# Batch 0 runs half a stage ahead of batch 1 through the last layers of an eight-layer kernel

## The reference, cut to what matters

```python
# L2x: 16 heads of 8, keys and values from 77 context rows, mask, softmax, then Wo and bias
x = x + tanh(g_xattn[2]) * _L2_xattn_ref(_layernorm(x), ctx, mask, Wq, Wk, Wv, Wo, bo)
# L2f: rows quantised by their own maximum, gate and up (512 wide), silu(gate) * up quantised by row, down
x = x + tanh(g_ffn[2]) * _L2_ffn_ref(_layernorm(x), w_gate, w_up, w_down)
# L3x: one head of 128, 77 context rows
x = x + tanh(g_xattn[3]) * _L3_xattn_ref(_layernorm(x), ctx, ctx, Wq, bq, Wk, bk, Wv, bv)
# L3f: the mean of a batch's rows picks one of 8 experts for the whole batch, then relu MLP 128-512-128
x = x + tanh(g_ffn[3]) * _L3_ffn_ref(_layernorm(x), Wr, br, W1, b1, W2, b2)
```

## Time and profile before

| | |
|---|---|
| time, median of 3 runs | 411.97 us (411.04 to 412.08) |
| the profiled execution | 415.34 us, of which the span of its instructions is 413.6 us |
| busy in the span | PE 295.0 us (71%), DVE 220.8 (53%), ACT 135.2 (33%), POOL 106.4 (26%) |
| mean granted TensorE clock | 0.796 |

### The profile page before, as it was taken

One profiled execution on the slowest core, in us unless ns is written; L12 is line 12 of the kernel. 1 busy time (PEld: TensorE's weight loads), 2 busy tenths in 40 slices (PEclk: granted clock), 3 DMA queues, 4 the chain that ended last, 5 costly groups with the idle time before them and its releaser, 6 DMA issues.

```text
span 413.6 us, 4876 instructions
## 1 busy us (share of the span) xinstructions
PE 295.0 (71%) x1699; PEld 230.0 (56%) x1699; DVE 220.8 (53%) x609; ACT 135.2 (33%) x242; POOL 106.4 (26%) x106
## 2 busy tenths in 40 slices
PE   2879979978858884566998053676999726475396
PEld 1659879568758873334898013233779513254245
DVE  4444542203161014788985369659987588825501
ACT  2220425823221221144443070134454348321150
POOL 4402217603235240224333100412445000000000
PEclk9755755999997898698999655599999966555589
DMA  8970004476765533091000000000000000000001
GB/s 217 339 164 1 0 12 144 155 203 179 238 201 161 175 105 108 3 360 44 0 2 2 0 1 0 0 0 2 1 2 0 2 0 0 1 2 0 0 0 52
DMA packets 21399, 29.72 MB, mean 72 GB/s; under 512 B 3521, under 2 KB 14223, under 8 KB 21376
## 3 DMA queue, kind: packets, MB, share of 16 engines
q1 hardware_dynamic: 19686, 26.66, 21.5%
q0 software_dynamic: 1312, 2.60, 1.9%
q10 hardware_dynamic: 378, 0.16, 0.3%
HBM read 24.74 MB, written 4.67 MB: 71 GB/s over the span
## 4 chain that ended last, share of the span: by engine, by line
PE 43%; DVE 28%; POOL 8%; issue 8%; DMA 7%; ACT 4%; SPq 1%; DVEq 0%; POOLq 0%; ACTq 0%
PE bank L1036 8%; DMA experts<-in_w 5%; POOL xg L558 4%; PE bank L813 4%; PE bank L986 4%; PE bank L978 3%; DVE ln L1210 3%; PE bank L1020 3%; POOL rstd L510 2%; PE bank L1175 2%; DVE pmax L1416 2%; DVE bn L1202 2%; DVE pr L1417 2%; PE bank L1184 2%; PE bank L1018 2%
## 5 line engine op out<-in xcount | busy, mean ns | idle before, releaser
L510 POOL TENSOR_TENSOR rstd<-var,minus_half 128x4 f32<-128x4 f32 x16 | 16.3, 1022 | 112.2 <-DVE var L1207 112.0
L546 POOL TENSOR_TENSOR pr<-pr,psums 128x1232 f32<-128x1232 f32 x12 | 27.0, 2249 | 54.2 <-DVE psums L1427 54.2
L595 ACT ACTIVATE prT<-bank 128x512 f32<-128x512 f32 (+1 forms) x48 | 22.1, 488 | 51.1 <-PE bank L813 50.8
L564 POOL DMA_INDIRECT yt<-acc,experts x23 | 22.5, 980 | 44.4 <-DVE acc L1396 43.0
L978 PE MATMUL bank<-prT,experts 128*128 128x128 f32 x184 | 26.6, 291 | 9.4 <-DMA experts<-in_w 8.7
L1396 DVE COPY acc<-bank 128x128 f32<-128x128 f32 x23 | 6.6, 291 | 46.7 <-PE bank L986 46.6
L1416 DVE TENSOR_REDUCE pmax<-bank 128x6 f32<-128x462 f32 (+1 forms) x48 | 27.4, 571 | 5.4 <-PE bank L1022 3.5
L797 PE MATMUL bank<-ident,ln 128*128 128x128 f32 x40 | 9.5, 383 | 29.1 <-DVE ln L1210 29.1
L978 PEld LDWEIGHTS bank<-prT,experts 128*128 128x128 f32 x184 | 24.0, 204 | 11.2 <-issue 11.2
L986 PE MATMUL bank<-experts,prT 128*128 128x128 f32 x184 | 26.7, 295 | 3.6 <-DVE acc L1396 3.6
L813 PE MATMUL bank<-ident,pr 128*128 128x128 f32 (+1 forms) x140 | 21.7, 290 | 8.2 <-POOL pr L546 7.9
(11 more groups left out here) (282 smaller groups left out, 628.6 us busy)
## 6 DMA issues: line engine op xcount, KB each, us to landing
experts<-in_w SPq DMA_DIRECT2D x23, 512.0 KB, 4.2
experts<-in_w SPq DMA_DIRECT2D x2, 2048.0 KB
xg<-experts SPq DMA_DIRECT2D x1, 1518.0 KB, 10.2
experts<-xg SPq DMA_DIRECT2D x5, 264.0 KB, 5.4
experts<-yt SPq DMA_DIRECT2D x4, 256.0 KB, 3.6
x<-in_x SPq DMA_DIRECT2D x2, 256.0 KB, 3.8
wkv<-in_wk SPq DMA_DIRECT2D x1, 512.0 KB, 6.7
wkv<-in_wv SPq DMA_DIRECT2D x1, 512.0 KB, 6.8
```

The costliest lines, as they stand in the source:

```text
L510: pool.tensor_tensor(rstd[:, b * TB:b * TB + TB], var[:, b, :], minus_half[:, :], ALU.pow).then_inc(rstd_ready, 1)
L546: pool.tensor_tensor(v, v, psums[:, n % 4, 1, :].unsqueeze(2).to_broadcast([P, H, R]), ALU.mult).then_inc(p_ready, 1)
```

## The change

Everything up to tile 5 of L2x stays as it is. From there the lists of all engines are written anew. VectorE does `finish_l2x(0)` before the sums of tile 7, then the four L2f tiles of batch 0, and only then `finish_l2x(1)`. L3x of batch 0 is threaded between the four L2f tiles of batch 1, and L3x of batch 1 between the steps of L3f of batch 0. `project(0)` moves ahead of the weighted values of tile 4. Buffers that would now be shared move: the Silu output and the gate-up product to `n1`, the attention weights of L3x to `m1` and their transpose to `wo1`, three tiles that are no longer read by then. The ordinal of a layer norm is now that of its place in the list `LN`. The number and size of matmuls, vector operations and transfers stay the same; ScalarE gets two more table loads. The diff, cut to the new order (`gate_up` on VectorE is the product, maximum and inverse of one tile, `gu_round` its rounding, `gu_scale` on ScalarE its scaling):

```diff
-LAYERS = ["L0x", "L0f", "L1x", "L1f", "L2x", "L2f", "L3x", "L3f"]
+LAYERS = ["L0x", "L0f", "L1x", "L1f", "L2x", "L2f"]
+LN = [(layer, b) for layer in LAYERS for b in range(B)] + [("L3x", 0), ("L3f", 0), ("L3x", 1), ("L3f", 1)]
...
+            if layer == "L2x" and n == T - 1:
+                t.append(("xqT", "L2f", 0))
             t += [("pT", layer, n, i) for i in range(len(TCH))]
             if n % TB == 0:
                 o.append((layer, n // TB))
-            if n % TB == TB - 1 and layer == "L2x":
-                o.append(("o2", n // TB))
+            if n == TB - 1 and layer == "L2x":
+                o.append(("o2", 0))
         if layer == "L1x":
             t += [("xqT", "L1f", b) for b in range(B)]
             s += [("h1", b, c) for b in range(B) for c in range(C)]
             o += [("L1f", b) for b in range(B)]
-    t += [("xqT", "L2f", b) for b in range(B)]
-    s += [(w, n) for n in range(T) for w in ("gate", "up")]
-    t += [("guT", n) for n in range(T)]
-    o += [("L2f", b) for b in range(B)]
-    t += [("lnT", "L3x", b) for b in range(B)]
-    s += [("s3", b) for b in range(B)]
-    t += [("aT3", b) for b in range(B)]
-    o += [("L3x", b) for b in range(B)]
-    t += [("lnT", "L3f", b) for b in range(B)]
-    s += [("pick", b) for b in range(B)]
-    s += [("h3", b, c) for b in range(B) for c in range(C)]
-    o += [("L3f", b) for b in range(B)]
+    o += [("L2f", 0), ("o2", 1), ("L3x", 0), ("L2f", 1), ("L3x", 1), ("L3f", 0), ("L3f", 1)]
+    s += [(w, n) for n in range(TB + 2) for w in ("gate", "up")]
+    s += [("s3", 0)]
+    s += [(w, n) for n in range(TB + 2, T) for w in ("gate", "up")]
+    s += [("pick", 0), ("s3", 1)] + [("h3", 0, c) for c in range(C)]
+    s += [("pick", 1)] + [("h3", 1, c) for c in range(C)]
+    t += [("guT", n) for n in range(TB)]
+    t += [("xqT", "L2f", 1), ("lnT", "L3x", 0), ("guT", TB), ("guT", TB + 1), ("aT3", 0)]
+    t += [("guT", n) for n in range(TB + 2, T)]
+    t += [("lnT", "L3f", 0), ("lnT", "L3x", 1), ("aT3", 1), ("lnT", "L3f", 1)]
...
-        silu = pr[:, :, 0:FF]
-        guf = prT[:, :, 0:C, :].rearrange("p n c k -> p n (c k)")
+        n1f = n1[:, :, :, :].rearrange("p b c d -> p (b c d)")
+        silu = n1f[:, 0:2 * FF].rearrange("p (n k) -> p n k", n=2)
+        guf = n1f[:, 2 * FF:4 * FF].rearrange("p (n k) -> p n k", n=2)
+        att3 = m1[:, :, :].rearrange("p b n -> p (b n)")[:, E * D:E * D + B * TB * R].rearrange(
+            "p (b t r) -> p b t r", b=B, t=TB)
+        attT3 = wo1[0:R, :, :].rearrange("r c d -> r (c d)").rearrange("r (b n) -> r b n", b=B)
...
+                    if layer == "L2x" and n == T - 1:
+                        inverse_root("L2f", [0])
...
-            for layer in ("L2f", "L3x", "L3f"):
-                inverse_root(layer)
+            inverse_root("L2f", [1])
+            for b in range(B):
+                inverse_root("L3x", [b])
+                inverse_root("L3f", [b])
...
+            exps("L2x", 0)
+            for n in range(T - 1):
+                attention_tile("L2x", n)
+                if n == TB:
+                    weighted_copy(0)
+            n = T - 1
+            quantised("L2f", 0)
+            gate_silu(0)
+            gate_silu(1)
+            p_copy("L2x", n, 0)
+            p_copy("L2x", n, 1)
+            gu_scale(0)
+            p_copy("L2x", n, 2)
+            gate_silu(2)
+            gu_scale(1)
+            gu_copy(0)
+            weighted_copy(1)
+            gate_silu(3)
+            gu_scale(2)
+            gu_copy(1)
+            gu_scale(3)
+            gu_copy(2)
+            gu_copy(3)
+            quantised("L2f", 1)
+            gate_silu(4)
+            gate_silu(5)
+            transposed("L3x", 0)
+            gu_scale(4)
+            gate_silu(6)
+            gu_scale(5)
+            gu_copy(4)
+            exp3(0)
+            gate_silu(7)
+            gu_scale(6)
+            gu_copy(5)
+            att3_copy(0)
+            gu_scale(7)
+            gu_copy(6)
+            gu_copy(7)
+            transposed_sum(0)
+            transposed("L3x", 1)
+            exp3(1)
+            relu(0, 0, 2)
+            att3_copy(1)
+            relu(0, 2, C)
+            transposed_sum(1)
+            relu(1, 0, C)
...
+                                if layer == "L2x" and n == TB + 1:
+                                    project(0)
                                 weighted(n - 1)
...
+                    if layer == "L2x" and n == T - 2:
+                        transpose_quantised("L2f", 0)
+                        gate_up(0)
+                        gate_up(1)
+                if layer == "L2x":
+                    gate_up(2)
                 weighted(T - 1)
...
+            transpose_gu(0)
+            gate_up(3)
+            project(1)
+            down(0)
+            for m in range(1, TB):
+                transpose_gu(m)
+                down(m)
+            transpose_quantised("L2f", 1)
+            gate_up(4)
+            gate_up(5)
+            transpose_rows("L3x", 0)
+            scores3(0)
+            transpose_gu(4)
+            gate_up(6)
+            down(4)
+            transpose_gu(5)
+            gate_up(7)
+            transpose_att3(0)
+            down(5)
+            values3(0)
+            for m in range(6, T):
+                transpose_gu(m)
+                down(m)
+            transpose_rows("L3f", 0)
+            pick(0)
+            transpose_rows("L3x", 1)
+            scores3(1)
+            last_up(0, 0, 2)
+            transpose_att3(1)
+            last_up(0, 2, C)
+            values3(1)
+            last_down(0)
+            transpose_rows("L3f", 1)
+            pick(1)
+            last_up(1, 0, C)
+            last_down(1)
...
+            attention("L2x", TB + 1)
+            less_max("L2x", TB + 2)
+            sums("L2x", TB + 1)
+            less_max("L2x", TB + 3)
+            sums("L2x", TB + 2)
+            finish_l2x(0)
+            sums("L2x", TB + 3)
+            gate_up(0)
+            gate_up(1)
+            gu_round(0)
+            gate_up(2)
+            gu_round(1)
+            gate_up(3)
+            gu_round(2)
+            gu_round(3)
+            finish_l2x(1)
+            finish_l2f(0)
+            gate_up(4)
+            gate_up(5)
+            gu_round(4)
+            softmax_in(("s3", 0), 0, att3)
+            gate_up(6)
+            gu_round(5)
+            softmax_out(0, B + 1, att3)
+            gate_up(7)
+            gu_round(6)
+            gu_round(7)
+            finish_l3x(0)
+            finish_l2f(1)
+            pick(0)
+            softmax_in(("s3", 1), 1, att3)
+            softmax_out(1, B + 2, att3)
+            finish_l3f(0)
+            finish_l3x(1)
+            pick(1)
+            finish_l3f(1)
```

More of the change, by code:

```diff
@@ L762, in _, with weighted_copy, gate_silu @@
-            for b in range(B):
-                transposed("L3x", b)
-            for b in range(B):
+            def weighted_copy(b):
+                copy_out(O, ("L2x", b), o2T[:, b, :], O.bank(("L2x", b))[:, :])
+            def gate_silu(n):
+                act.wait_ge(tscale_ready, n // TB + 1)
+                if n >= 2:
+                    act.wait_ge(*S.freed(("up", n - 2)))
+                act.wait_ge(*S.filled(("gate", n)))
+                act.activation(silu[:, n % 2, :], S.bank(("gate", n))[:, :], ACT.Silu,
+                               scale=tsc[:, 2, n:n + 1]).then_inc(S.free(("gate", n)), 1)
@@ L767, in _, with att3_copy, transposed_sum @@
[L767 to L770 removed]
+                act.activation(att3[:, b, :, :], att3[:, b, :, :], ACT.Exp, scale=D ** -0.5).then_inc(att_exp, 1)
+            def att3_copy(b):
+                copy_out(TR, ("aT3", b), attT3[:, b, :], TR.bank(("aT3", b))[0:R, :])
+            def transposed_sum(b):
                 key = ("lnT", "L3f", b)
@@ L1084, in attention, with project @@
-                if layer == "L2x":
-                    project(1)
+                    if layer == "L2x" and n == T - 2:
[4 more added lines that the diff above has]
+                    gate_up(2)
+                weighted(T - 1)
+            def project(b):
+                bank = acquire(O, ("o2", b))
+                pe.wait_ge(*O.freed(("L2x", b)))
+                for t in range(TB):
+                    o = bank[:, t * D:t * D + D]
+                    ins = pe.matmul(o, o2T[:, b, t * P:t * P + P], w2x[:, 3, :], start=True, stop=True)
+                ins.then_inc(O.full(("o2", b)), 1)
@@ new lines, in pick, with last_up @@
+            def pick(b):
+                bank = acquire(S, ("pick", b))
+                pe.wait_ge(*lnT_done("L3f", b))
+                pe.wait_ge(*loaded("l3f"))
+                pe.matmul(bank[0:1, 0:E], sum3[:, b:b + 1], wr3[:, :], start=True, stop=True).then_inc(S.full(("pick", b)), 1)
+            def last_up(b, c0, c1):
+                pe.wait_ge(pick_ready, b + 1)
+                for c in range(c0, c1):
+                    bank = acquire(S, ("h3", b, c))
```

(23 more changed lines are left out.)

325 lines of the change are left out of this document (123 added, 202 removed).

## The result

The changed kernel takes 418.02 us (median of 4 runs, 417.47 to 418.5); the kernel before, on the same chip, takes 411.5 us (median of 4, 408.71 to 412.08). The ratio is 1.0145, with a 95% interval of 1.0101 to 1.0189: slower by 6.0 us (4.2 to 7.8). The prediction said 415.8, with a range of 410.0 to 420.5 and 0.66 for slower.

A forecast was written before the change was run, and what follows sets the result against it. Four stages with four limits: VectorE idle at the second attention's end, VectorE-bound L2f, a chain of short steps in L3x, TensorE-bound L3f. 0 + 11.0 - 7.2 = +3.8 on the 411.97 median gave 415.8 us, range 410.0 to 420.5.

The forecast's parts named there:

- First term: From tile 5 of L2x to the end of finish_l2x(1): idle stretch filled, waits elsewhere; change 0, ending at 344.75.
- The walk: Steps through the new engine lists with old-trace durations from tile 5 of L2x, against the profiled span of 413.6 us.
- the price that was listed as unknown: TensorE's clock at tile 7, with little work between 319.7 and 325.2: 0 to +2.5 us, taken as 0.
- Second term: To the end of finish_l2f(1): 19.6 us plus moved-in work 6.6, waits 4.1, handing over 0.3; 11.0 later than 364.3.
- The prediction's sign for this part: Two table loads around the Exp, VectorE waiting on ScalarE there, finish_l2f(1) ending 10 to 12 us later than 364.3.
- The table loads: Two added loads around batch 0's L3x Exp: nothing to 2.6 us, about 1.8 on the path, no added drain.
- Third and fourth part: From the end of finish_l2f(1) to the kernel's end: 42.1 us where the old kernel needs 49.3, a gain of 7.2.
- rival 3: TensorE's clock stays low through batch 0's L3f: up to +7.3 us, 423, with 419.5 likelier; chance 0.14.
- The fourth part: From the end of batch 0's L3f matmuls to the end, VectorE's list decides: 24.9 us, ending at 417.4.
- TensorE's gap: Expected sign: TensorE idle for over 9 us between batch 0's down products and batch 1's hidden pieces, chain through L1640.
- Rival 2: TensorE's clock comes up early, from batch 1's scores on: 5.5 to 6.9 us less, 408.9 to 410.3; chance 0.19.
- Rival 4: Waits between finish_l2x(1) and the end of finish_l2f(1) vanish, 4.4 us: 411.3, or 413.5 with half; chance 0.17.

The follow-up runs named there:

- experiment 1: Changed kernel with batch 1's L3x update and norm ahead of batch 0's last L3f update in VectorE's list: 420.43 us, ratio 1.0011 to the kernel before.
- experiment 5: Changed kernel plus 32 added matmuls with unread results, filling TensorE's idle time in the last 25 us: 423.91 us, ratio 1.0061 to the kernel before.
- experiment 3: Changed kernel with L3x's exponential replaced by Silu, so no table loads after the first Silu: 425.24 us, ratio 1.013 to the kernel before.
- experiment 6: Kernel of experiment 1 plus 11 added matmuls, 10 of them ahead of batch 1's hidden pieces: 418.59 us, ratio 0.996 to the kernel before.
- experiment 2: Changed kernel with all lists in the old order up to the end of both L2x updates: 425.93 us, ratio 1.0132 to the kernel before.
- experiment 9: Kernel of experiment 7 run once more, unchanged: 412.74 us, ratio 0.9871 to the kernel before.
- experiment 7: Changed kernel with all lists reordered after the first part so ready steps don't stand behind waiting ones: 419.53 us, ratio 0.9873 to the kernel before.

## Why the prediction was right

**First term (0; measured +1.0).** The walk's order of events held: the start of `finish_l2x(0)` and the end of tile 7's sums (321.08 + 1.78 = 322.9, as walked), then waits for Silu. Some 0.3 us were lost before TensorE came to tile 7 (the first wait, 1.88 for 1.6). The rest is the price that was listed as unknown, TensorE's clock at tile 7 (0 to +2.5, taken as 0): it fell to half, 0.69 over 324 to 328. `finish_l2x(1)` ended at 343.91 + 1.78 = 345.7, where 344.75 was walked and 344.7 is old. Taking the row of before (dense at 1.00) for a stretch behind 6 us of which TensorE works 2.1 was the weaker choice. The price also varies: the weighted values behind tile 7's first transposes took 2.99 and 3.01 us in the two traces of the changed kernel, 3.18 and 3.19 in experiments 1 and 5, and 4.05 and 4.15 in 3 and 6, with the same lists up to there. So the first term is +1.0 to +2.1.

**Second term (11.0 with the start at 344.75; measured 12.5, of which 1.0 is the first term's).** 31.1 us for 30.6. The waits were 5.4 us (1.41, 0.72, 0.70, 1.43, 0.61, 0.57) for 4.1: a wait for tile 6's Silu was missing (0.72), and tile 7's product waited 1.43 for 0.75. The work between them, handing over included, was 0.8 us less than counted, so two errors partly cancel here. The prediction's sign for this part, 10 to 12 us later than 364.3, was missed by 0.5. The table loads: the walk had 1.8 us of 2.6 on the path, experiment 3 has 1.28. Silu begins at 360.83, 0.02 us behind the end of its load (359.53 + 1.28), and Exp at 358.48 in the same way, so nothing like a drain stands behind a load here. Nor does it stand ahead of one: the first load begins at 357.19, 0.03 us behind the end of the copy before it (356.58 + 0.58). The Trainium skill ("ScalarE: Activation LUTs", section "What ACT_TABLE_LOAD costs") has 1.38 us of drain for each; the trace doesn't agree with that, and going by the row was right.

**Third and fourth part (-7.2; measured -7.8).** From 375.03 to the end of batch 0's down products are 17.1 us for 17.2 (the parts listed add up to 17.3). The clock came up where the walk took it to (0.69 in 382 to 386, 1.00 after), which was the choice between the forecast and rival 3. The fourth part took 24.4 us for 24.9: the last hidden pieces 5.12 and the down products at the full clock. The wait of L1640 was 9.06 us and TensorE's gap 10.0 us, of which it was idle for 8.7 where over 9 was expected. Experiment 1 shows that the order of two entries of VectorE's list holds most of the loss against the kernel before: batch 1's values were ready at 387.3 (L1190) and were taken at 392.81.

**The sum.** 1.0 + 0.5 - 0.1 - 0.5 = 0.9 us more than +3.8: the tail's +4.7, which two traces of each kernel give to 0.03 us. On the median of 411.97 that is 416.7. The ratio says 6.0, and its interval (4.2 to 7.8) holds 4.7. The 1.3 us between may be executions in which the last stretch ran as in experiments 1 to 3 (2.9 us longer), or in which the clock at tile 7 came up as late as in experiments 3 and 6 (1.1 us longer). Neither trace of the changed kernel shows one, so this is argued and stays open.

**The rivals.** Rival 2 fell: the clock is 0.50 over all of 344 to 375, and batch 1's scores, from 377.04 on, took their 1.36 + 1.99 us at it. TensorE was busy without a pause from there, and the clock rose only at 384 to 385 (0.75 there, 1.00 in the next), behind the scores. The Trainium skill's rule that work without a pause raises it ("TensorE: Matmul & The Clock Gate", section "What's actually happening") agrees with the rise, but it came later than this rival needed. Rival 3 fell, since the clock was up in time for batch 0's down products (3.84 us at 1.00). Rival 4 fell, since the waits that were to vanish were 5.4 us.

## What to carry to other kernels

When two independent streams share engines whose lists are fixed, look at each list for a ready step of one stream that stands behind a waiting step of the other, and price it by the wait in the bracket: here the order of two lines of VectorE's list was worth 5.5 us of a 6.0 us loss by the ratios, and 2.7 us of 4.7 by the traces, or 5.6 with the clock of the last stretch as before. A gap on TensorE costs its length and then the clock: the same hidden pieces took 5.12 to 6.58 us behind the gap, and 3.70 with the gap filled. And compare two traces from the last point that they share, since the shared layers alone moved by 5.8 us between two executions of the old kernel, and what follows them by 0.01.

## What the runs showed of the hardware that I had not expected

TensorE's clock fell inside work without a gap. In experiment 9 it went from 1.00 to 0.50 at 391, a good microsecond into 32 down products in which TensorE is busy for 1.00 us of every 1.00, and the 32 took 5.47 us instead of 3.84. The last 32 took 5.46 or 5.47 us there and in experiments 1 to 3, 5 and 7, and 3.84 in both traces of before, in both of the changed kernel and in experiment 6. Ahead of it TensorE had short gaps (in experiment 9 it was busy for 0.36 us of the 1.00 from 388 to 389). The order of TensorE's list does not decide it alone: the changed kernel and kernel 3 have the same, and the last down products took 3.84 us twice in the one and 5.46 in the other. What does decide it is not settled. It means that 1.6 us per batch at the end can't be planned for.
